# Earlier router biases and weight copies, six norm buffers, and longer runs of second-layer tiles beside each gelu, in an attention and mixture-of-experts kernel

## The reference

```python
xn = layernorm(x)
p = xn @ Wv.T + bv                       # q = k = v = p, 16 heads of 8
attn = softmax(p @ p.T / sqrt(8)) @ p    # per batch and head
s = attn @ Wo.T + bo
z = layernorm(xn) * ln_g + ln_b
probs = softmax(z @ rW + rb)             # 8 experts; the best two kept and scaled to sum 1
hid = gelu(z @ W1[e] + b1[e])            # for the two experts of each token
mixed = sum_e w_e * (hid @ W2[e] + b2[e])
out = x + s * silu(xn + mixed)
```

## Time and profile before

| | |
|---|---|
| three runs | 638.78, 642.05 and 642.69 us, median 642.05 |
| profiled execution | 640.8 us, of which the trace's span is 639.1 |
| PE busy | 565.0 us, 88% of the span |
| ACT busy | 545.1 us, 85% |
| DVE, POOL busy | 234.8 us (37%), 228.8 us (36%) |
| mean granted TensorE clock | 0.928 of 2.4 GHz |

### The profile page before, as it was taken

The page is one execution under the profiler, slowest core; times in us unless marked ns, Lnnn a source line. Parts: engine busy times, 40 slices in busy tenths (PEclk is TensorE's granted clock), DMA queues, the critical chain, the costliest instruction groups (busy, mean ns, idle before and its releaser), DMA issues.

```text
span 639.1 us, 11460 instructions
## 1 busy us (share of the span) xinstructions
PE 565.0 (88%) x3982; PEld 227.1 (36%) x3982; DVE 234.8 (37%) x663; ACT 545.1 (85%) x597; POOL 228.8 (36%) x252
## 2 busy tenths in 40 slices
PE   3888389863699999979999999999997979999995
PEld 2642024210234344343444443434334334443321
DVE  5740786830233333212232222322232562222383
ACT  6879188854499999999999999999999969999994
POOL 2571047777777730047312221122103234342000
PEclk9978589878699999959999999999995989999998
DMA  6367941276454665434444435444333545351221
GB/s 162 123 199 218 412 157 51 76 185 180 102 119 99 144 149 114 101 90 119 102 129 112 138 79 143 102 119 117 91 120 103 137 136 162 110 158 55 77 73 40
DMA packets 101557, 81.54 MB, mean 128 GB/s; under 512 B 54083, under 2 KB 92502, under 8 KB 100694
## 3 DMA queue, kind: packets, MB, share of 16 engines
q1 hardware_dynamic: 94838, 71.26, 41.3%
q0 software_dynamic: 6656, 9.48, 4.5%
HBM read 57.03 MB, written 28.39 MB: 134 GB/s over the span
## 4 chain that ended last, share of the span: by engine, by line
PE 67%; DVE 8%; issue 7%; ACT 7%; DMA 6%; SPq 3%; POOL 2%; ACTq 0%; DVEq 0%
PE bank_v L1350 32%; PE pair L1298 15%; PE bank_f L1399 9%; PE bank_f L1390 8%; ACT exps L800 6%; DMA p_dram<-o_ring 2%; PE bank_f L1367 1%; DMA bo_bc<-in_L_attn_bo 1%; POOL o_ring L668 1%; DMA p_dram<-w_ring 1%; PE bank_f L1363 1%; DMA rows_in_sb<-o_dram 1%; DMA rows_in_sb<-in_L_attn_bv 1%; PE bank_f L1374 1%; DVE rows_in_sb L837 1%
## 5 line engine op out<-in xcount | busy, mean ns | idle before, releaser
L800 ACT ACTIVATE exps<-pair 128x1024 f32<-128x1024 f32 x512 | 489.7, 1051 | 75.2 <-PE pair L1298 57.2
L1350 PE MATMUL bank_v<-exps,v_tok 128*32 128x512 f32 x2048 | 285.5, 631 | 15.9 <-DVE o_turned L1103 15.0
L695 POOL DMA_INDIRECT o_dram<-o_ring,slot_place x80 | 77.1, 964 | 260.3 <-DVE o_ring L1154 259.7
L1298 PE MATMUL pair<-q_ring,k_ring 26*128 26x512 f32 x1024 | 153.1, 516 | 3.7 <-ACT exps L800 1.8
L1298 PEld LDWEIGHTS pair<-q_ring,k_ring 26*128 26x128 f32 x1024 | 60.6, 188 | 99.0 <-ACT exps L800 53.4
L680 POOL DMA_INDIRECT z_dram<-pre,dest_i x64 | 63.3, 989 | 55.0 <-DVE place_i L1058 35.8
L1399 PE MATMUL bank_f<-w_ring,pre 128*128 128x128 f32 x320 | 63.0, 325 | 13.6 <-ACT pre L776 5.5
L1399 PEld LDWEIGHTS bank_f<-w_ring,pre 128*128 128x128 f32 x320 | 46.6, 210 | 76.0 <-issue 42.4
L1390 PEld LDWEIGHTS bank_f<-zT,w_ring 128*128 128x128 f32 x320 | 42.5, 193 | 84.4 <-DVE pre L1145 43.4
L1390 PE MATMUL bank_f<-zT,w_ring 128*128 128x128 f32 x320 | 57.7, 304 | 16.2 <-issue 16.2
L1145 DVE TENSOR_TENSOR pre<-bank_f,w_ring 128x256 f32<-128x256 f32 x80 | 33.9, 423 | 104.0 <-PE bank_f L1390 102.2
(11 more groups left out here) (156 smaller groups left out, 269.5 us busy)
## 6 DMA issues: line engine op xcount, KB each, us to landing
w_ring<-w_dram SPq DMA_DIRECT2D x80, 192.0 KB
w_ring<-w_dram SPq DMA_DIRECT2D x80, 129.0 KB
q_ring<-p_dram SPq DMA_DIRECT2D x64, 104.0 KB
k_ring<-p_dram SPq DMA_DIRECT2D x64, 96.0 KB
z_dram<-s_tok SPq DMA_DIRECT2D x4, 1280.0 KB, 13.1
z_ring<-z_dram SPq DMA_DIRECT2D x80, 64.0 KB
rows_in_sb<-o_dram SPq DMA_DIRECT2D x16, 256.0 KB, 3.0
p_dram<-z_ring SPq DMA_DIRECT2D x12, 256.0 KB, 3.1
```

The lines of the kernel that those rows point to most:

```text
L695: pool.indirect_dma_start(o_dram[:, :], bass.IndirectOffsetOnAxis(slot_place[:, h, 4 * k + i:4 * k + i + 1].bitcast(U32), 0), o_ring[:, q ...
L800: nc.scalar.activation(exps[:, g % ES, 2 * half:2 * half + 2, :], pair[(2 * g + half) % 3][:, :, :], ACT.Exp, scale=SCALE).then_inc(exp_do ...
L1298: ins = nc.tensor.matmul(pair[h % 3][:, j % 2, :], k_ring[32 * j:32 * j + KROWS, n % 2, kt * P:(kt + 1) * P], q_ring[32 * j:32 * j + KROWS ...
L1350: ins = nc.tensor.matmul(bank_v[32 * j:32 * j + 32, :], v_tok[:, (n // HG) * KT + kt, first:first + 32], exps[:, g % ES, j, :], start=(kt ...
```

## The change

- **Biases.** The loads of the router's bias `rb` and of the attention's `bo` move on SP from behind the loads of unit 1 to right behind those of x.
- **Router and bias steps.** Half 0's rank, count, assign, scale, exponential and weigh steps stand two steps earlier, its scatter too (13). The four bias uses move from steps 22, 23, 25, 26 to 13 to 16, the scaling of W1 from 27 to 30 to 17, 18, 20, 22, so its store to DRAM stands at step 23 (before 31).
- **Norms.** The six norm uses move from 27, 28, 30, 31, 33, 34 to 25, 26, 28, 29, 31, 32 and go to six separate buffers (the free `p_hi`, `p_lo` and `m_blk`), so DVE waits for no store between them. SP waits for all six stores ahead of `load_z(0)`.
- **Copies.** `keep_w2` and `clear_places` move from step 38 to 10, the DRAM copy of the hi rows (L594) from 14 to 16.
- **Mixture.** First slot at 39 (41). Slots 1.26 steps apart (1.19): from steps 97 to 186, 80 of 90 steps have a use (84). The burst has 12 downs, three quads (six, and two more later). The gelus stand at steps 94 and 190 (92 and 188), the last down at 230 (232).
- **Loads.** In each of SP's steps `load_w2` and `load_rows` come first, and the weights of a quad that lies in a burst are asked for right ahead of its first down. `combine` begins three steps after `LOAD_AT` (two).

The diff, cut to its core:

```diff
@@ -84,24 +84,25 @@
-RANK_AT = ((6, 6, 7, 7, 8, 8), (17, 18, 19, 20, 22, 23))
-COUNT_AT = (11, 24)
-ASSIGN_AT = ((11, 12, 12, 13, 14), (25, 26, 27, 28, 30))
-SCALE_Z_AT = ((9, 10, 10, 11), (18, 20, 22, 23))
-EXP_AT = (14, 21)
-WEIGH_AT = ((15, 15, 16), (31, 32, 33))
-BIAS_AT = 22
-COPY_HI_AT = 14
+RANK_AT = ((4, 4, 5, 5, 6, 6), (17, 18, 19, 20, 22, 23))
+COUNT_AT = (9, 24)
+ASSIGN_AT = ((9, 10, 10, 11, 12), (25, 26, 27, 28, 30))
+SCALE_Z_AT = ((7, 8, 8, 9), (18, 20, 22, 23))
+EXP_AT = (12, 21)
+WEIGH_AT = ((13, 13, 14), (31, 32, 33))
+BIAS_AT = 13
+COPY_HI_AT = 16
+KEEP_W2_AT = 10
 BIAS_COLS = 4
-NORM_AT = 27
+NORM_AT = 25
 ZERO_AT = 8
-SCALE_W1_AT = (27, 28, 29, 30)
-SCATTER_AT = (15, 36)
-MOE_AT = 41
-MOE_STEP = 1.19
+SCALE_W1_AT = (17, 18, 20, 22)
+SCATTER_AT = (13, 34)
+MOE_AT = 39
+MOE_STEP = 1.26
 LOAD_LAG = 5
-PLACE_AT = (59, 82)
-BURST = 6
+PLACE_AT = (57, 80)
+BURST_QUADS = 3
 SILU_TILES = 4
@@ -133,13 +134,9 @@
             g += 1
-        downs = [("down", first + i // 4, i % 4) for i in range(8)]
-        uses[g] = downs[:BURST]
+        uses[g] = [("down", first + i // 4, i % 4) for i in range(4 * BURST_QUADS)]
         at.update({what: g for what in uses[g]})
-        t = g + 3
-        for what in downs[BURST:]:
-            t = max(t, place(what, t) + 1 - MOE_STEP) + MOE_STEP
-        return g, t
+        return g, g + 3
@@ -155,11 +152,12 @@
     for k in range(2, QUADS):
-        t = both("down", k, t)
+        if k >= BURST_QUADS:
+            t = both("down", k, t)
         t = both("up", QUADS + k, t)
...
     gelu.append(second)
-    for k in range(2, QUADS):
+    for k in range(BURST_QUADS, QUADS):
         t = both("down", QUADS + k, t)
@@ -173,7 +171,7 @@
 TURN_Z_AT = [AT["up", q, 0] - 1 for q in range(HALVES * QUADS)]
-COMBINE_AT = [[g + 2 + i * 3 // 4 for i in range(HT)] for g in LOAD_AT]
+COMBINE_AT = [[g + 3 + i * 3 // 4 for i in range(HT)] for g in LOAD_AT]
 SILU_AT = [COMBINE_AT[c * SILU_TILES // HT][c * SILU_TILES % HT + SILU_TILES - 1] + 2 for c in range(SILUS)]
@@ -327,7 +325,8 @@
         parts_stored = [sem(f"parts_stored{i}") for i in range(2)]
-        m_kept = [sem(f"m_kept{i}") for i in range(3)]
+        m_kept = sem("m_kept")
+        later_kept = sem("later_kept")
         m_row_ready = sem("m_row_ready")
@@ -386,6 +385,10 @@
+        def later_norms(g):
+
+            return (p_hi, p_lo, m_blk)[(g - EARLY) // 2][0:H, g % 2:g % 2 + 1, :]
+
         x_v = x.rearrange("b s d -> (b s) d").rearrange("(t p) d -> p t d", p=P)
@@ -417,6 +420,8 @@
                 load_x(c)
+            sp.dma_start(rb_bc[:, :], rb.rearrange("(a d) -> a d", a=1).broadcast_to([P, E])).then_inc(bias_in, 16)
+            sp.dma_start(bo_bc[:, :], bo.rearrange("(a d) -> a d", a=1).broadcast_to([P, D])).then_inc(bias_in, 16)
             sp.wait_ge(zeros_ready, 1)
@@ -463,8 +468,7 @@
                     sp.wait_ge(hi_copied, 32)
-                    for i in range(2):
-                        sp.wait_ge(m_kept[1 + i], (NB - EARLY) // 2 * 16)
+                    sp.wait_ge(later_kept, (NB - EARLY) * 16)
                 load_keys(n)
@@ -478,18 +482,16 @@
                         sp.wait_ge(n2_copied, e + 1)
-                        sp.dma_start(p_dram[:, M_ROW, e * BLK:(e + 1) * BLK], m_blk[:, e, :]).then_inc(m_kept[0], 16)
+                        sp.dma_start(p_dram[:, M_ROW, e * BLK:(e + 1) * BLK], m_blk[:, e, :]).then_inc(m_kept, 16)
                     for e in range(EARLY):
...
                     load_keys(0)
-                    sp.wait_ge(m_kept[0], 16 * EARLY)
+                    sp.wait_ge(m_kept, 16 * EARLY)
                     sp.wait_ge(m_zeroed, 32)
...
             load_unit(1)
-            sp.dma_start(rb_bc[:, :], rb.rearrange("(a d) -> a d", a=1).broadcast_to([P, E])).then_inc(bias_in, 16)
             sp.dma_start(w1_stage, W1.rearrange("e h f -> h e f")).then_inc(w1_staged, 16)
-            sp.dma_start(bo_bc[:, :], bo.rearrange("(a d) -> a d", a=1).broadcast_to([P, D])).then_inc(bias_in, 16)
             zero_z(0)
@@ -500,7 +502,7 @@
                 sp.wait_ge(bank_f_read, written("norm", g))
-                sp.dma_start(p_dram[:, bass.ds(m_row, 1), g * BLK:(g + 1) * BLK], m_blk[:, g % 2:g % 2 + 1, :]).then_inc(m_kept[1 + g % 2], 16)
+                sp.dma_start(p_dram[:, bass.ds(m_row, 1), g * BLK:(g + 1) * BLK], later_norms(g)).then_inc(later_kept, 16)
@@ -550,6 +552,8 @@
                 h, k = divmod(q, QUADS)
+                if q == 0:
+                    sp.wait_ge(later_kept, (NB - EARLY) * 16)
                 if k == 0:
@@ -587,6 +591,13 @@
                 n, k = divmod(g, US)
+                for q in range(HALVES * QUADS):
+                    if g == (min(AT["down", q - 2, 3] + 1, AT["down", q, 0]) if q >= 2 else MOE_AT + 16 + 6 * q):
+                        load_w2(q)
+                for h in range(HALVES):
+                    for i in range(0, HT, LOAD_TILES):
+                        if g == LOAD_AT[h] + i * 3 // 4:
+                            load_rows(h, i)
                 if k == VLAG and 1 <= n < NU - 1:
@@ -602,22 +613,17 @@
                     zero_z(1)
-                if g == SCATTER_AT[1] + 2:
+                if g == KEEP_W2_AT:
                     keep_w2()
...
                         load_places(h)
-                    for i in range(0, HT, LOAD_TILES):
-                        if g == LOAD_AT[h] + i * 3 // 4:
-                            load_rows(h, i)
                 for q in range(HALVES * QUADS):
...
                         load_w1(q)
-                    if g == (AT["down", q - 2, 3] + 1 if q >= 2 else MOE_AT + 16 + 6 * q):
-                        load_w2(q)
                 for n in range(NU - 1):
@@ -1126,11 +1132,11 @@
                     g = arg[0]
-                    if g < EARLY + 2:
-                        dve.wait_ge(m_kept[0], 16 * EARLY)
-                    else:
-                        dve.wait_ge(m_kept[1 + g % 2], (g - EARLY) // 2 * 16)
-                    ins = nc.vector.tensor_scalar(m_blk[:, g % 2, :].bitcast(F32R), bank_f[0:H, :], -1.0, None, ALU.mult)
+                    if g == EARLY:
+                        dve.wait_ge(m_kept, 16 * EARLY)
+                        for i in range(2):
+                            dve.wait_ge(parts_stored[i], stored(NB - 2 + i))
+                    ins = nc.vector.tensor_scalar(later_norms(g).rearrange("h a n -> h (a n)").bitcast(F32R), bank_f[0:H, :], -1.0, None, ALU.mult)
                 elif what == "count":
```

## The result

The changed kernel takes 623.27 us (618.91 to 624.39, four runs) beside 641.65 us for the kernel before: a ratio of 0.971, 95% interval 0.965 to 0.976. The forecast was 619. The profiled execution took 623.62 us, 17.2 less than that of before; the trace's span is 621.9.

The account below looks back on a forecast made before the run. PE bounds from 173 to 270 us; the early part is held by late arrivals. -32.2 + 20.4 - 5.5 - 4.8 = -22.1 gives 618.7 by profiled time, 620.0 by median; forecast 619, own range 613 to 627, wider 605 to 631.

Parts of the forecast that it names:

- The early part: Up to the first ups: earlier biases, separate norm buffers and moved copies leave 14.5 of ACT's 46.7 us waiting, -32.2 us.
- The first quad's waiting: At step 39 PE waits 5.7 us for the first quad of z, 8 with the slow steps behind it.
- The bias uses: At steps 13 to 16 they wait behind DVE's assign; 4 us of waiting kept, bias matmuls included.
- The bursts: At both gelus, six added downs, 1.66 us apart at clock 0.50, delay the next scores; weights 0.2 late: +20.4 us.
- Rival B: The bursts run at 2.4 GHz, downs 1.06 us apart: +11.4 instead of +20.4, 609.7 us; chance 0.12.
- Here the trace disagrees: Against the skill's warm engine across DVE copies: with only DVE's reads between downs, the clock stays at 0.50.
- Fewer uses: Between the bursts, twelve downs leave the slots, each saving 0.46 us of a step: -5.5 us.
- The stop at the combine: Near 516 ACT waits 5.0 us; gathers first on SP and a later combine remove it: -4.8 us, between 0 and -5.0.
- Prices of nothing: Earlier bias loads priced at nothing, 1 us without cover; copies at 62 covered by unit 2's distance, at most 11.97 us late.
- C: The first quad comes 10 us later than forecast: early gain 22, about 629 us; chance 0.15.
- D: Copies fill the DMA queues, the first quad is turned no earlier than 164.2, no early gain: 654.6 us; chance 0.05.

Follow-up runs that it names:

- Experiment 4: The changed kernel with the four bias uses at steps 17, 18, 20, 22 and the scaling of W1 at 23 to 26: 617.20 us, ratio 0.962.
- experiment 1: The changed kernel with the old burst of six downs, two more later, and slots 1.19 steps apart: 607.67 us, ratio 0.946.
- kernel 5: The changed kernel with each burst's 12 downs written by PE in quads, each quad read by one DVE instruction: 610.75 us, ratio 0.952.
- 11: The kernel of experiment 1 with the gathers back behind SP's other loads and the combine two steps behind them: 612.42 us, ratio 0.952.
- 7: The changed kernel with the edits of experiment 1 and Experiment 4, but eight downs per burst, written and read by quads: 603.44 us, ratio 0.944.
- 9: Kernel 7 with the first two quads of z asked for at step 34 instead of 36: 598.36 us, ratio 0.931.
- 10: Kernel 5 with bias uses at 17 to 22 and the first quads of z asked for at step 34: 600.66 us, ratio 0.933.
- kernel 2: The changed kernel with the copies of W2 and b2 and the clearing of the places back at step 36: 634.31 us, ratio 0.987.

## Why the prediction was right, point by point

- **The early part, forecast -32.2, measured -27.7.** This term was mis-sized, within the ends that were given for it (22 to 37): ACT's waits were 19.5 where 14.5 were to stay. The mechanism held: undoing the copies cost 11 us (2), undoing the bias loads 12 (3). The first quad's waiting was 9.0 where 8 was forecast. Its turning came at 133.30 where 128 was: the way from the last norm use (113.87) to the end of the turning took 20.1 where 18.8 was added up, and the rest fits the delay of the bias uses. The bias uses were the failing step: "With the bias matmuls themselves I keep 4 us of waiting", and they took 8.6. The first bias was read at 72.36, as foreseen near 71. What I left out was the clock behind the wait: PE stood 1.52 us, the clock fell to the lower level, and three steps took 4.2 to 4.4 us each. Experiment 4 shows it by taking the wait away: clock 1.00, and 6.9 us back.
- **The bursts, forecast +20.4, measured +20.9.** Downs 1.67 apart at 0.50, weights 0.3 and 0.6 late; the two waits of ACT, 10.32 and 10.60, make the same sum, and experiment 1 takes them away. Rival B (2.4 GHz) is refuted for this kernel by the windows. It is not out for other forms of the burst: written by quads, two of three quads in kernel 5's second burst ran at 1.00. So the prediction's "Here the trace disagrees" says more than its rows show (see 5). That the figures agree to half a microsecond is luck in part. The forecast left out the steps behind a burst at half clock, which experiment 5 puts at 2.1 us for the first, and the table's two stretches hold three of the uses that fell away.
- **Fewer uses, forecast -5.5, measured -5.5** (what is left of the table between the other terms: 1.5, 2.5, 0.4 and 1.1). This is a remainder and not a measurement of the term: in those stretches ten steps fewer have a use by the timetable, 4.6 us at the forecast's 0.46.
- **The stop at the combine, forecast -4.8, measured -5.4.** The size was right, the reason is shown only for the kernel before. There the order and the later combine remove it (12); in the changed kernel undoing both does not bring it back (8). So in the change the size is luck as far as the reason goes.
- **Prices of nothing.** The early biases: the first step began 1.06 us later (42.79 for 41.73), which is within what the eleven traces with early biases show (41.14 to 42.92), and the fifth on a level with before (50.61 for 50.66). The copies at 62: SP issued for 24 us instead of 11, and unit 2's loads at 88.50 were in time.
- **Rivals C and D** did not come: the first quad was 5 us later than thought, not 10, and the scatter went at its old pace (half 0 from 72.68 to 111.92).

The terms, -27.7 + 20.9 - 5.5 - 5.4 = -17.7 against -22.1, add up to the table's last row, as the third is its remainder.

## What to carry to other kernels

Work that is put beside a stop on another engine pays only as long as that stop lasts: six downs fitted the gelu, and the other six cost their full 10 us at each gelu, more than half of what the rest of the change gained. When a use is moved earlier, look at what its reader has queued ahead of it, and count the slower clock behind a wait as well as the wait. And a time that falls into a theory's range does not show its mechanism: in runs 5 and 11 only the rows said which cause had acted, and in run 5 only the rows of both bursts, as the first shows one clock and the second another.

## What the runs showed of the hardware

A wait of 1.52 us on PE between short bias matmuls was followed by some 14 us at a granted clock of 0.52, while PE was busy 13.73 of 14.0 us there. In kernel 4 the same matmuls, without the wait, ran at 1.00.

Behind PE's stop of 2.74 us for the gelu, with DVE's read behind each down, the changed kernel's bursts ran at 0.50 to their end. Written by quads, with a read of 0.95 us behind each quad, the clock was not the same in every burst of one execution: in kernel 5's first burst the first two quads took 3.8 us each, at 0.50, and in its second 2.0, at 1.00. Of the eight such bursts in the traces of kernels 5, 7, 9 and 10, four have a quad of 2.0 us.

Issuing two copies of W2 took SP 2.92 us late in the program and 16.43 us at 62, right behind the zeroing of `z_dram`, where the DMA engines were already 90% busy in the kernel before. In kernel 2, late again, they took 2.79. A move to an earlier place can make the same instruction several times as long on the queue that issues it.
